# Gate and up products of a Macaron block by one Strassen level, weights streamed from DRAM

## The reference, cut to what matters

```python
def ffn(x, W1, W2, W3):              # x [512, 512], W1 and W3 [2048, 512], W2 [512, 2048]
    hidden = silu(x @ W1.T) * (x @ W3.T)
    hidden = fwht(hidden)            # Walsh-Hadamard transform over the 2048
    return hidden @ W2.T

x = x + 0.5 * ffn(layernorm(x), W1, W2, W3)
x = x + attention(layernorm(x), ...) # 16 heads of 32, ternary qkv and proj weights, chunks of 128
x = x + 0.5 * ffn(layernorm(x), W1, W2, W3)
```

## Time and profile before

| what | value |
|---|---|
| median of the runs | 2472.5 us |
| the profiled execution | 2471.01 us |
| its span, first to last instruction | 2469.3 us |
| TensorE matmul | 2380.9 us busy, 96%, 13040 instructions |
| VectorE | 1188.8 us, 48% |
| ScalarE | 720.9 us, 29% |
| GpSimd | 161.8 us, 7% |
| chain that ended last | TensorE 87%, VectorE 5%, DMA 3%, issue 3% |
| DMA | 158.07 MB, 229410 packets |
| mean granted TensorE clock | 0.987 |

### The profile page before, as it was taken

One profiled execution on the slowest core, in us unless ns is written; L12 is line 12 of the kernel. 1 busy time (PEld: TensorE's weight loads), 2 busy tenths in 40 slices (PEclk: granted clock), 3 DMA queues, 4 the chain that ended last, 5 costly groups with the idle time before them and its releaser, 6 DMA issues.

```text
span 2469.3 us, 32106 instructions
## 1 busy us (share of the span) xinstructions
PE 2380.9 (96%) x13040; PEld 1147.9 (46%) x13040; DVE 1188.8 (48%) x2087; ACT 720.9 (29%) x1205; POOL 161.8 (7%) x111
## 2 busy tenths in 40 slices
PE   6688899999999999999999999999999999999999
PEld 2243454455444544455444554445444554445444
DVE  6766456535453453543535355444535345444512
ACT  5545332322222321233213322232212232233211
POOL 4720000000000000000000000000000000000000
PEclk9899999999999999999999999999999999999999
DMA  8633223212321031202212123111222112211200
GB/s 221 166 95 98 73 61 95 47 43 73 69 49 46 22 107 35 66 29 78 64 40 56 43 73 68 35 44 39 84 58 52 43 46 66 52 61 53 75 19 18
DMA packets 229410, 158.07 MB, mean 64 GB/s; under 512 B 171024, under 2 KB 195600, under 8 KB 226192
## 3 DMA queue, kind: packets, MB, share of 16 engines
q1 hardware_dynamic: 229264, 156.03, 23.6%
HBM read 73.15 MB, written 41.94 MB: 47 GB/s over the span
## 4 chain that ended last, share of the span: by engine, by line
PE 87%; DVE 5%; issue 3%; DMA 3%; ACT 1%; SPq 1%; POOL 0%; POOLq 0%; DVEq 0%; ACTq 0%
PE d_bank L1366 25%; PE l_bank L1351 24%; PE g_bank L1351 24%; PE a_bank L1407 4%; PE a_bank L1393 2%; PE a_bank L1474 2%; PE a_bank L1461 2%; PE a_bank L1425 1%; PE a_bank L1455 1%; DMA parts_dram<-q_parts 1%; PE a_bank L1439 1%; DMA w1t<-cent 1%; DMA work<-parts_dram 0%; DVE work L1056 0%; DMA xt<-cent 0%
## 5 line engine op out<-in xcount | busy, mean ns | idle before, releaser
L1366 PE MATMUL d_bank<-w2t,work 128*128 128x512 f16 x2976 | 685.5, 381 | 5.6 <-DVE work L1063 5.6
L1056 DVE SCALAR_TENSOR_TENSOR work<-l_bank,l_scale,work 128x512 f32<-128x512 f32 x256 | 191.9, 750 | 664.8 <-PE l_bank L1351 664.7
L1366 PEld LDWEIGHTS d_bank<-w2t,work 128*128 128x128 f16 x2976 | 288.9, 98 | 342.4 <-DVE work L1063 6.1
L1351 PE MATMUL l_bank<-xt,w3t 128*128 128x512 f16 x1728 | 406.7, 386 | 28.6 <-DVE work L1056 28.6
L1351 PE MATMUL g_bank<-xt,w1t 128*128 128x512 f16 x1728 | 401.9, 383 | 7.0 <-DMA w1t<-cent 5.5
L808 ACT ACTIVATE work<-g_bank,g_scale 128x512 f32<-128x512 f32 x256 | 175.5, 686 | 613.3 <-PE g_bank L1351 606.6
L821 ACT CAST work<-work 128x512 f16<-128x512 f32 x248 | 153.2, 618 | 565.3 <-DVE work L1056 564.5
L1351 PE MATMUL g_bank<-work,w1t 128*128 128x512 f16 x1344 | 308.4, 379 | 0.0
L1351 PE MATMUL l_bank<-work,w3t 128*128 128x512 f16 x1344 | 308.4, 379 | 0.0
L1351 PEld LDWEIGHTS l_bank<-xt,w3t 128*128 128x128 f16 x1728 | 170.1, 99 | 237.1 <-issue 44.8
L1351 PEld LDWEIGHTS g_bank<-xt,w1t 128*128 128x128 f16 x1728 | 169.2, 99 | 211.1 <-issue 8.4
(11 more groups left out here) (179 smaller groups left out, 1605.3 us busy)
## 6 DMA issues: line engine op xcount, KB each, us to landing
work<-parts_dram SPq DMA_DIRECT2D x192, 128.0 KB, 2.6
x_dram<-work SPq DMA_DIRECT2D x16, 1024.0 KB, 4.4
w2t<-in_L_ffn_W_dram SPq DMA_DIRECT2D x32, 256.0 KB, 3.3
xin<-in_L_attn_x_dram SPq DMA_DIRECT2D x8, 1024.0 KB, 7.6
parts_dram<-q_parts SPq DMA_DIRECT2D x32, 256.0 KB, 2.0
parts_dram<-k_parts SPq DMA_DIRECT2D x32, 256.0 KB, 2.1
work<-x_dram SPq DMA_DIRECT2D x8, 1024.0 KB, 4.8
work<-x_dram SPq DMA_DIRECT2D x28, 256.0 KB, 4.0
```

Source lines behind the costliest of these rows:

```text
L1056: nc.vector.scalar_tensor_tensor(out=hfull, in0=l_bank[:], scalar=l_scale[:, j:j + 1], in1=gate, op0=ALU.mult, op1=ALU.mult).then_inc(hful ...
L1351: ins = nc.tensor.matmul(dst[:], wt[:, wp, k, P * j:P * (j + 1)], src[:, xp, k, :], start=(k == 0 and wp == xp), stop=(k == KT - 1 and wp ...
L1366: ins = nc.tensor.matmul(d_bank[t][:], parts[:, hp, P * t:P * (t + 1)], w2t[:, wp, j, :], start=(j == 0 and hp == wp), stop=(j == HT - 1 a ...
```

## The change

- W1 and W3 are multiplied by one Strassen level (Winograd's form). Two hidden tiles are a pair; the pair's 256 x 512 weights and the 512 x 512 activations are cut into quadrants. Seven products of 128 hidden x 2 blocks, K = 256 and 256 tokens take the place of eight. Each is 6 matmuls with 256 columns (`product`).
- The activations are stored as seven operands (B22, B11, B21, T1 to T4), formed by VectorE in the norm (`pprep`, `comb`, `half`, `low2`).
- The weights' seven operands of each pair and matrix are formed in the first FFN by f32 matmuls with scaled diagonal matrices (`make`), split in high and low, kept in a ring of 15 slots of 256 KB, and written to `w_dram`. From the second FFN on all weights, W2's too, are loaded from `w_dram` into the ring, 72 units an FFN, by the queue of SyncE.
- Sums of products are formed partly by accumulation in PSUM, with snapshots by ScalarE and additions by VectorE between them. A later product in the same bank waits for these.
- The hidden results of all 16 tiles stay in SBUF (`hid`); the W2 products of an FFN follow in a second phase. There are two sets of three banks, used alternately, which also hold the W2 sums.
- The attention and the norms are laid out anew, in units of which 28 of 42 lie in the first phase of an FFN and 14 in the second.

The core of the diff, the order of steps first, then the branches of each engine (the attention's branches are the same but for their bookkeeping):

```diff
+        def feed_forward(n, slots, fill=True):
+            steps = [("begin", n), ("zx", (0, 0)), ("zx", (1, 0)), ("y", 0)]
...
+            for p in range(PAIRS):
+                last = p == PAIRS - 1
+                steps += [("u", p)] + ([("cast", p - 1)] if p else []) + slot()
+                if not last:
+                    steps += [("zx", (0, p + 1))]
+                elif fill:
+                    steps += [("down", (0, RES_ORDER[1:]))]
+                steps += slot() + ([("low", p - 1)] if p else []) + [("h", p)] + slot()
+                if not last:
+                    steps += [("zx", (1, p + 1))]
...
+                steps += slot() + [("last", (0, p))] + slot()
+                if not last:
+                    steps += [("y", p + 1)]
...
+                steps += slot() + [("last", (1, p))] + slot() + [("mult", p)]
+            steps += [("cast", PAIRS - 1), ("low", PAIRS - 1)]
+            if fill:
+                steps += [("down", (j, RES_ORDER[:1])) for j in range(3)] + slot()
+                for j in range(3, HT):
+                    steps += [("down", (j, RES_ORDER))] + slot()
+                steps += [("resid", t) for t in RES_ORDER]
+            return steps
...
+            def put(unit, steps):
+                n, r = 1 + unit // 42, unit % 42
+                add(slots, (n, 2 * r if r < 28 else 28 + r), steps)
```

SyncE, the load of one unit, two steps after its slot's last use:

```diff
+            def load_unit(i):
+                slot = i % RING
+                sp.wait_ge(*consumed(i - RING))
...
+                sp.dma_start(ring[:, slot], w_dram[source]).then_inc(u_loaded[slot], 16)
```

TensorE:

```diff
+            def product(dst, unit, which, operand, start):
+
+                weights_of = unit.rearrange("p (a b k h) -> p a b k h", a=2, b=2, k=2)
+                for k in range(2):
+                    for wp, xp in ((0, 0), (0, 1), (1, 0)):
+                        ins = nc.tensor.matmul(dst, weights_of[:, wp, which, k, :], f.x[:, operand, xp, k, :],
+                                               start=(start and k == 0 and wp == xp), stop=(k == 1 and wp == 1),
+                                               skip_group_check=True)
+                return ins
...
+                elif step == "zx":
...
+                    elif p >= 2:
+
+                        pe.wait_ge(x_read[m], pair - 1)
+                    unit = arrived(POSITION[n, (step, m, p)])
+                    product(banks[m][:, 0:HALF], unit, 0, B21, True)
+                    product(banks[m][:, HALF:], unit, 1, B11, False).then_inc(zx_ready[m], 1)
...
+                elif step in ("u", "h"):
...
+                    for m in range(2):
+                        pe.wait_ge(copied_out[m], pair + 1)
+                        product(banks[m][:, HALF:], unit, m, operand, False).then_inc(done[m], 1)
+                elif step == "last":
...
+                    pe.wait_ge(snap_u3[m], pair + 1)
+                    product(banks[m][:, HALF:], unit, 0, T4, False)
+                    for read in ((c12_done[0],) if m else c22_done):
+                        pe.wait_ge(read, pair + 1)
+                    product(banks[2][:, HALF * m:HALF * (m + 1)], unit, 1, B22, False).then_inc(k_ready[m], 1)
```

ScalarE:

```diff
+                elif step == "zx":
...
+                    if n and p < 2 and not m:
+                        act.wait_ge(res_done, TT * n)
+                    nc.scalar.copy((gate, lin)[m][:, s, 0, 0:HALF], banks[m][:, HALF:]).then_inc(snap_p1[m], 1)
...
+                elif step == "h":
...
+                    for m in range(2):
+                        act.wait_ge(h_ready[m], pair + 1)
+                        nc.scalar.copy((gate, lin)[m][:, s, 1, HALF:], banks[m][:, HALF:]).then_inc(snap_u3[m], 1)
...
+                elif step == "cast":
+                    p = arg
+                    act.wait_ge(hfull_ready, PAIRS * n + p + 1)
...
+                    nc.scalar.copy(hid[:, 2 * p:2 * p + 2, 0, :], lin[:, p % 2]).then_inc(hi_ready, 1)
```

VectorE:

```diff
+                elif step == "h":
...
+                    for m in range(2):
+                        dve.wait_ge(snap_u3[m], pair + 1)
+                        c22 = (gate, lin)[m][:, s, 1, HALF:]
+                        nc.vector.tensor_tensor(c22, banks[2][:, HALF * m:HALF * (m + 1)], c22, ALU.add).then_inc(c22_done[m], 1)
...
+                elif step == "low":
+                    p = arg
+
+                    dve.wait_ge(hi_ready, PAIRS * n + p + 1)
+                    tiles = hid[:, 2 * p:2 * p + 2]
+                    nc.vector.tensor_tensor(tiles[:, :, 1, :], lin[:, p % 2], tiles[:, :, 0, :], ALU.subtract).then_inc(lo_ready, 1)
```

More of the change, by code:

```diff
@@ L103, in macaron_kernel @@
         x2_dram = nc.dram_tensor("x2_dram", [2, P, TT, D], F32, kind="Internal").ap()
[L104 to L111 removed]
+        w_dram = nc.dram_tensor("w_dram", [7 * PAIRS + HT, P, 4 * HALF], F16, kind="Internal").ap()
@@ L373, in macaron_kernel, with units_of @@
-        WITH_LAST_ATTENTION = feed_forward(0, "ffn2", last_slots())
-        LAST = feed_forward(0, "ffn2", {10: [("back", 0)]})
+                steps += [("down", (j, RES_ORDER))] + slots.get(j, [])
+            return steps + [("resid", t) for t in RES_ORDER], units
+        FIRST, FIRST_UNITS = first_steps()
+        REST = rest_steps()
+        def units_of(steps):
+            order_of = []
+            for step, arg in steps:
+                if step in UNIT_STEPS:
+                    order_of.append(unit_key(step, arg))
+                elif step == "down" and ("w2", arg[0]) not in order_of[-20:]:
+                    order_of.append(("w2", arg[0]))
+            return order_of
@@ new lines, in macaron_kernel, with consumed @@
+        for i in range(PER, len(STREAM)):
+            seen[i % RING] += 1
+            LOADS[i] = seen[i % RING]
+        def consumed(i):
+            n, name = i // PER, STREAM[i]
+            kind, p = name[0], name[-1]
+            if kind in ("zx", "last"):
+                return (zx_ready if kind == "zx" else k_ready)[name[1]], PAIRS * n + p + 1
+            if kind in ("u", "h"):
+                return (u_ready if kind == "u" else h_ready)[1], PAIRS * n + p + 1
+            if kind == "y":
+                return y_ready, PAIRS * n + p + 1
+            if p == HT - 1:
+                return d_ready, TT * (n + 1)
+            return d_step, DOWN_STEPS[n, p]
@@ new lines, in filled, with copied, __init__, norm_source @@
+        def filled(step, arg):
+            return USES[step, arg]
+        def copied(step, arg, b):
+            return COPIED[step, arg][b]
+        class FeedForward:
+            def __init__(self, n):
+                self.n = n
+                self.which, self.batch = next((kind, b) for kind in ("ffn1", "ffn2") for b in range(B) if order(kind, b) == n)
+                self.x = xt if n == 0 or n % 2 else yt
+                self.source = NORM[self.which, self.batch]
+        def norm_source(key):
+            kind, b = key
+            if kind == "ffn1":
+                return {1: x_next, 2: x1}.get(b, xin)
+            return x1 if kind == "qkv" else x2
```

2072 lines of the change are left out of this document (1079 added, 993 removed).

## The result

The changed kernel takes 2640.8 us (median of 4 runs, 2638.85 to 2641.51) against 2472.6 us: a ratio of 1.068 [1.066, 1.070]. It is 168 us slower. The forecast had slower as the likeliest, at 2530 us, but the time lies 111 us above it and 11 us over the end of the range.

The account below looks back on a forecast made before the run. TensorE's instruction stream was taken as the bound. First stage 300 + 14 x 150.5 + last FFN 8 x 9.7 + 41.5 + end and outside 6 = 2532, forecast 2530 us, range 2385 to 2630.

Parts of the forecast that it names:

- Products at 0.110 us: Gate and lin products: matmuls of 256 columns 0.110 us between starts, 9.2 us a pair, 145 us less for 128 pairs.
- the spacing rule: Trainium skill's rule: weight load and matmul both set spacing; half-size matmuls pay some 25 ns each, 270 us, cancelling the gain.
- So it waits 0.5 us in every pair, even in the last FFN: TensorE in last(gate) waits 0.5 us for VectorE's C22 adds without any attention work, making a pair 9.7 us.
- VectorE's sum: VectorE's busy time over the whole kernel goes from 1189 to about 1620 us, most of the added work in first phases.
- The wait for the C22 adds with attention: First phase of FFNs with attention: TensorE waits 3.5 us at every second pair, 0.7 in the other; phase 100 us, not 90.
- 150.5 us an FFN, against 148 now: Each of 14 FFNs with attention: first phase 100 us, second 49.5, start 1; bounds 139.5 and 163.
- 56 waits at 1.45 us: Clock rival: each 3.5 us wait, four an FFN, lowers TensorE's clock; +80 us, 2610 in all; chance 0.09.
- 18 us, and with the butterflies on GpSimd beside it, ... 20 to 24; I take 23: First stage, a pair: VectorE needs 18 us, 20 to 24 beside GpSimd, TensorE's own 21.5; taken at 23.
- less what is made ahead: First stage: pairs end at 32 + 8 x 23 = 216, less weights made ahead; the whole stage taken at 300 us.
- about 12 us of waiting for ternary weights: First stage's W2 products: TensorE waits about 12 us, as inputs load only after the last store (8.63 before).
- W2's turning, 33: First stage, behind the pairs: W2's turning takes 25 us as before, plus 8 for a scale chain that was hidden.
- The stream at nothing: Weight loads from the second FFN on cost nothing, queue at 66%; rival of a late stream 2610 to 2650, chance 0.05.

Follow-up runs that it names:

- early rows: Changed kernel with loads of the second batch's x and four parameter rows issued amid the first stage's products, not behind the last weight store: 2634.2 us, 1.066.
- short butterflies: Changed kernel with each of GpSimd's 32 butterfly operations cut in four over a quarter of the columns, same total work: 2617.0 us, 1.059.
- split: Changed kernel with VectorE's second half of each score step (wait for ScalarE's cast, then subtraction) moved one slot later: 2610.9 us, 1.057.
- distribution: Changed kernel with 24 attention and norm units in an FFN's first phase and 18 in the second, instead of 28 and 14: 2603.2 us, 1.054.
- light scores: Changed kernel with three quarters of VectorE's part in the 128 score steps left out (one head of four masked and subtracted): 2603.1 us, 1.054.
- the combination: Changed kernel with low part later, score step in two, loads earlier, units 24 and 18, and butterflies in quarters, all together: 2574.9 us, 1.041.

## Why the prediction was right in its direction and wrong in its size

- **Products at 0.110 us**: 0.109, right; the spacing rule that spoke against the change (270 us) did not show. A pair without attention is 9.2 us. The last FFN takes 120.4 us against 119.
- **"So it waits 0.5 us in every pair, even in the last FFN"**: half of it, 0.22 us in every pair of the last FFN but the first. VectorE's instructions follow one another at 0.33 us (1978.09, 1978.42, and the next at 1978.76) where the count took 0.42 for each: durations of VectorE overlap too, and the rule that it used for TensorE, distance of starts and not duration, holds here as well. The same goes for VectorE's sum: 1620 was expected, 1543 measured.
- **The wait for the C22 adds with attention**: right in place and cause. It is the first line of the waits, up to 4.4 us ("3.5"). TensorE's idle time in the middle, 162/14 = 11.6 us an FFN, is near the count's 10 in the first phase and 1 at the start. That the two sums agree is in part luck: the waits behind it (snapshots by ScalarE, 25; the later adds, 12; `l_bank` and the second phase) hold over half of the sum, and the regular pattern, 3.5 us in every second pair and 0.7 in the others, is not there: 50 waits in the 112 pairs of the middle, 1.2 us in the mean.
- **"150.5 us an FFN, against 148 now"**: 155.2, and 150.5 before, from the windows. This is the step that failed in the middle, 66 of the 111 us by which the forecast missed. By the table above an FFN has 138.7 us of TensorE's own time (the sum had 139.5) and 11.6 of idle time (11), so both stand. The 4.7 us are two terms that the sum put at nothing: 2.2 us of delays that no idle time shows, like the 0.22 above, and 2.7 us lost in stretches at the lower clock. The second was a rival ("56 waits at 1.45 us", chance 0.09) and came at about half of that price, on top of the forecast's other terms and not instead of them. (The 148 was low for another reason: it spread 28 us of idle time outside the attention; the whole middle before should have been read as one window.)
- **What the clock costs**, more exactly: no experiment changed it alone, but the kernels whose edits lie in the first stage have the same middle, and their clocks differ. With early rows the middle has 61 us at the lower level, loses 28.5 us by it, is idle for 168.1 and takes 2168.7; with short butterflies it has 92 us, loses 42.5, is idle for 160.4 and takes 2172.9. So 14 us more of loss made the whole only 4 us longer: a slower TensorE waits less for the others. The 38.5 us are an upper bound, and without them the waits would likely have been over the forecast. Of the clock, the Trainium skill ("TensorE: Matmul & The Clock Gate", section "HAM oscillation — how this bites in real kernels") tells of a kernel that waits for its data before each piece of work and starts every piece at the lower clock; the trace agrees in kind, in 20 places and not behind every wait.
- **"18 us, and with the butterflies on GpSimd beside it, ... 20 to 24; I take 23"**: this is the step that failed in the first stage. A pair takes 26.9 us; over eight pairs that is 31 of the 45 us by which the first stage missed. Another 6.5 are a credit in the same sum: its terms add up to 306.5 and it took 300 "less what is made ahead", but the 28 matmuls made ahead of 33.30 (6.2 us) are already left out of the 26.9. The price of the butterflies was read as a ratio (0.69 to 1.14) on a mean of VectorE instructions, in which those that met no GpSimd instruction hide what the others pay. Each of those shown above with all inputs in SBUF that meets one pays up to 2.3 us, whatever its size, and the scale chain is a row of the smallest. Without the butterflies the pair takes 22.9 us, near 21.5, TensorE's own; in pieces of a quarter they give back two thirds.
- **"about 12 us of waiting for ternary weights"**: 19.2, right in kind; 6.5 of it by the late load. The stretch behind W2's turning takes 67 us, 10 over its 57.5: 7 by this wait, 2 by the matmuls at the lower clock behind it.
- **The start, 32**: 33.3. **W2's turning, 33**: 29.2. Both near.
- **The stream at nothing**: right, 0 us by the kernel without it; the share of the queue was 59.4%, 66% expected.

The first stage was 45 us over, the middle 66, the last FFN 1. The direction came right by the two parts that were forecast: the first stage longer, the gain of the products taken up by waits. The range failed since its upper end was built from single bad cases, and here two came together; the first stage's own upper bound (330) was itself passed by 15.

What stays open: why the middle's edits don't add. Each of split, distribution and light scores reaches 2133 to 2138 us and the combination as well, which looks like a second bound, but they get there by different parts: idle time 138, 142, 131 and 142 us, lower clock 68, 41, 78 and 55 us. ScalarE's snapshot is no such bound by these runs, since with units 24 and 18 its wait is 14.0 us and in the combination 30.4, at the same time of the middle.

## What to carry to other kernels

A product made cheaper by adding operations on other engines is paid for in their order, more than in their sums: follow one tile's chain through every in-order queue, and then expect that a wait taken out at one link reappears, in part, at the next. Read what GpSimd does to VectorE by single instructions side by side in the timeline, never as a mean stretch, and keep GpSimd's instructions short where VectorE has small ones to do. Price waits of some microseconds with the slow clock behind them, since behind a wait of 4.4 us 30 matmuls lost another 2.9, but take off what the other engines catch up meanwhile. And where many short matmuls wait often, add up distances of starts: here 30 us of delays stood in no list of waits.

## What the runs showed of the hardware that was not expected

- A VectorE instruction of 128x2 took 2.31 us beside GpSimd, where its like took 0.15 us, and one of 128x256 with an input in PSUM took 0.47 us beside it. The same GpSimd work in instructions of 0.7 instead of 2.4 us cost the kernel 13 us instead of 37.
- 463 MB through one queue at 59% share in 256 KB units, 3.7 us to landing, against 180 MB at 25%: no difference in time (2640.1 and 2640.8 us).
- f16 matmuls of 256 columns, each with weights of its own, follow at 0.109 us, right between 0.057 at 128 and 0.216 at 512 columns.
- The same matmuls of the middle had between 61 and 92 us at the lower clock in the profiled executions of six kernels that differ only in the first stage or the loads, and took 2169 to 2176 us.
